# Decoding FP4 weight codes during attention and keeping the scales out of the gate and up products

## The chip, the cores and the metric

The kernel runs on one core of a Trainium2 chip. The metric is the device time of one execution in microseconds (us), as the median of several runs. The core has five engines with queues of their own, in order: TensorE (PE, matmuls), VectorE (DVE), ScalarE (ACT), GpSimd (POOL) and SyncE (SP, which here issues all DMA transfers). They wait for each other through semaphores.

## What is computed

`x` is (16, 100, 512) and the context (16, 361, 512), in float32. First a gated cross attention, then a gated feed-forward network (FFN) with FP4 weights:

```python
x = x + tanh(g_xattn[0]) * xattn(layernorm(x), ctx, mask, norm_w, wq, wk, wv, wo, wg)
x = x + tanh(g_ffn[0]) * ffn(layernorm(x), gate_up_packed, gate_up_scales, down_packed, down_scales)

def ffn(x, ...):                       # I = 1408 hidden, 512 in and out
    w_gu = dequant(gate_up_packed) * scale per (group of 128 inputs, output)
    w_down = dequant(down_packed)  * scale per (group of 128 hidden, output)
    gate, up = split(x @ w_gu.T)
    h = silu(gate) * up
    y = h @ w_down.T
    return y / sqrt(mean(y * y) + 1e-6)
```

A packed word holds eight 4-bit codes with the values 0, 0.5, 1, 1.5, 2, 3, 4, 6 and their negatives. The scales are float16.

## The kernel before

**Precision.** Matmuls run in a float32 format of TensorE with a shorter mantissa. Each operand is therefore kept as two halves, "hi" (rounded, made by ACT) and "lo" (the rest, made by DVE or POOL), and `product` (L254 to L258) issues three matmuls for each tile of 128 inputs: hi with hi, hi with lo, lo with hi (`PASSES`).

**Attention.** The 16 batches go in four groups of four. A group has 16 steps, one per head. `step` exists on PE (L1314), ACT (L689), DVE (L915) and POOL (L548), and each engine goes through its own list in the written order. On DVE a step is: split of the transposed probabilities (`probsT_lo`), normalising of the head before (`attn_norm`), row maxima two steps ahead (`row_max`), layer statistics of the next group in steps 6 to 9, splits of the projections that PE computes beside this step (`job_lo`, or `output` for the jobs O), normalising. The list `BESIDE` says which jobs stand beside which step: X (transposed input), Q, K, A and B (values), T (transposed head outputs), G (gate), O (output projection). Step 12 has X2, X3 and Q0 of the next group, and Q0 needs all X splits. The steps run in a loop over the first three groups (from step 6 of one group to step 5 of the next); the last ten steps, of the fourth group, are written out behind it, followed by T3, O0 to O3 and four `output` calls (L904 to L912), each of which ends in a tile of x1 that SP stores in DRAM (L393) and needs a residual tile `xa` that SP loads (L376).

**FP4 weights.** 17 pieces: 11 of gate and up (one hidden tile each, 128 gate and 128 up columns) and 6 of down. `decode` (L977 to L1023) has five stages, all on DVE: cut the scale (L992, L1011), shift the words (L995, L1000, L1003), take the magnitude (L1014), put in the sign (L1018), and multiply the codes, read as float16, by the two parts of the scale (L1021 for hi, L1023 for lo). Pieces 0 to 8 are decoded in steps 7 to 15 of the last group (`EARLY_AT`), the others between the hidden tiles of the FFN's first token group.

**FFN.** 1,600 tokens in five token groups of 320. Per token group: statistics and normalising of x1 on DVE (L1032 to L1046), transposing on PE (L1343), splitting into `mT` hi and lo (L727, L1053); then 11 hidden tiles, each with two products of 12 matmuls (`gate_up`, L1435), tanh on ACT (L799), gating and multiplication by up on DVE (`hidden_tile`, L1170 and L1173, both reading a PSUM bank), hi on ACT (L803), lo on POOL (L606). Then `down` (L1450): two or three tiles of up to 128 tokens, each with 11 x 3 matmuls of 512 columns, a square with sum on ACT (L810), mean on DVE (L1181), reciprocal root on POOL (L612), scale and residual on DVE (L1184, L1188). Gate and up use two pairs of banks in turn. PE does the down tiles of a token group between two groups' gate and up products. ACT waits for all of x1 to be stored after the first token group.

Of the kernel before, what the change touches and what calls it, by code (L numbers as in the profile page):

```python
# [9 lines left out]
ALU = mybir.AluOpType  # L10
# [3 lines left out]
B, L, D = 16, 100, 512  # L14
# [4 lines left out]
NB = 4  # L19
# [24 lines left out]
PAIRS = (FGROUPS - 1) // 2  # L44


OUT_TILES = ((64, ((64, 128),)), (192, ((192, 128),)), (0, ((0, 64), (TG, 64))), (128, ((384, 128),)), (256, ((512, 128),)))
TILES_OF = ((0, 1), (2, 3, 4))
FP4_UNIT = 16384.0
MASKED = 1e30  # L50
PIECES = FT + 6
# [3 lines left out]
def build(nc, x, ctx_tail, ctx_full, mask, mask_tail, g_xattn, g_ffn, norm_w, wq, wk, wv, wo, wg,  # L55
          gu_packed, gu_scales, dn_packed, dn_scales, identity, shifts, x1_dram, out):
    es = ExitStack()
    with es:
# [8 lines left out]
        shift = sb(es, "shift", [128, 5], I32)  # L67
# [52 lines left out]
        gate = [sb(phase_a, f"gate{b}", [L, D], F32) for b in range(NB)]  # L120
        phase_a.close()

        words = [sb(phase_b, f"words{s}", [128, D], I32) for s in range(2)]
        scale = [sb(phase_b, f"scale{s}", [128, D], F16) for s in range(2)]
        scale_a = [sb(phase_b, f"scale_a{s}", [128, D], F16) for s in range(2)]
        scale_b = [sb(phase_b, f"scale_b{s}", [128, D], F16) for s in range(2)]
        fp4 = [sb(phase_b, f"fp4_{s}", [128, D], I32) for s in range(2)]

        wgu = [[sb(phase_b, f"wgu{t}_{half}", [128, KT, 256], F32R) for half in ("hi", "lo")] for t in range(FT)]
        xb = sb(phase_b, "xb", [128, 3, D], F32)  # L130
        mT = [sb(phase_b, f"mT_{half}", [128, KT, TG], F32R) for half in ("hi", "lo")]
        hT = [sb(phase_b, f"hT_{half}", [128, FT, TG + 64], F32R) for half in ("hi", "lo")]
        tgate = sb(phase_b, "tgate", [128, TG], F32)
        hidden = [sb(phase_b, f"hidden{s}", [128, TG], F32) for s in range(2)]
        wdn = [[sb(phase_b, f"wdn{c}_{half}", [128, 2 if c < 5 else 1, D], F32R) for half in ("hi", "lo")] for c in range(6)]
        mn = [sb(phase_b, f"mn{m}", [128, D], F32) for m in range(3)]

        yo = [words[s][:, :].bitcast(F32) for s in range(2)]
        xr = [fp4[s][:, :].bitcast(F32) for s in range(2)]
# [12 lines left out]
        s_shift = sem("shifts_loaded")  # L152
# [39 lines left out]
        s_words = [sem(f"words_loaded{s}") for s in range(2)]  # L192
        s_scale, s_scaleb, s_shifted = sem("scale_cut"), sem("scale_last_bit"), sem("codes_shifted")
        s_dec = sem("piece_decoded")
        s_whi, s_wlo = sem("ffn_weight_hi"), sem("ffn_weight_lo")
# [4 lines left out]
        s_gu, s_tg, s_sg, s_h, s_hhi, s_hlo = (sem(n) for n in ("gate_up_ready", "tanh_gate", "silu_gate", "hidden_ready", "hidden_hi", "hidden_lo"))  # L200
        s_y, s_sq, s_ms, s_rr, s_cy, s_yo = (sem(n) for n in ("y_ready", "y_squared", "mean_square", "rrms_ready", "coef_ready", "out_ready"))
# [12 lines left out]
        def words_loaded(n):  # L214

            return sum(16 * (4 if m < FT else (5 if m - FT < 5 else 2)) for m in range(n % 2, n + 1, 2))

        def piece_operands(n, half):
            codes, factor = fp4[n % 2][:, :].bitcast(F16), (scale_a if half == HI else scale_b)[n % 2]
            if n < FT:  # L220
                out_ap = wgu[n][half][:, :, :].rearrange("p (two r) c -> p two r c", two=2)
                code = codes.rearrange("p (r c two) -> p two r c", r=2, two=2)
                factor = factor[:, 0:256].unsqueeze(1).unsqueeze(1).broadcast_to([128, 2, 2, 256])
                return out_ap, code, factor
            tiles = 2 if n < PIECES - 1 else 1
            code = codes.rearrange("p (c two) -> p two c", two=2)
            return (wdn[n - FT][half][:, :, :], code[:, 0:tiles, :],
                    factor[:, :].unsqueeze(1).broadcast_to([128, tiles, D]))

        def tile_bank(par, m):  # L230

            return bank[4 + m] if m < 2 else bank[2 * par + 1]

        def hidden_cols(par):

            return slice(64 * par, 64 * par + TG)

        def tile_rows(i, last):
            return 64 if last and i == 2 else 128

        def tile_transfers(h, i, last=False):

            tiles = [m for m in range(i % 2, len(OUT_TILES), 2)]
            per_pair = sum(len(OUT_TILES[m][1]) for m in tiles)
            upto = sum(len(OUT_TILES[m][1]) for m in tiles if m <= i)
            return per_pair * h + (upto - 1 if last and i == 2 else upto)
# [35 lines left out]
        EARLY_AT = {i: i - 7 for i in range(7, STEPS)}  # L282
        EARLY = len(EARLY_AT)
# [67 lines left out]
        def _(sp):  # L351
# [21 lines left out]
            sp.dma_start(shift[:, :], shifts).then_inc(s_shift, 16)  # L373

# [13 lines left out]
            def outputs(g, last):  # L388
                for b in range(NB):
                    if last and b < 3:  # L390
                        load_piece(EARLY - 1 + b)
# [5 lines left out]
                    elif not last:  # L397
                        load_residual(g + 1, b - 2)

            def load_piece(n):  # L400
                s = n % 2
                if n >= 2:
                    sp.wait_ge(s_scaleb, n - 1)
                    sp.wait_ge(s_dec, n - 1)
# [1132 lines left out]
```

## Time and profile before

| | us |
|---|---|
| median of 3 runs | 723.25 (722.58 to 727.46) |
| time of the profiled execution | 725.4 |
| its span, first to last instruction | 723.5 |
| PE busy | 636.1 (88%) |
| DVE busy | 374.2 (52%) |
| ACT busy | 224.6 (31%) |
| POOL busy | 110.9 (15%) |

The span runs from the first to the last instruction of the profiled execution. A row of a group of instructions gives their total and mean duration; engines work side by side, so busy times don't add up to the span. The chain of waits is the sequence of work that ended last, followed back from the end. Matmuls are pipelined: one lasts longer than the distance to the next, so that the chain's time over its count is what one costs. "PEclk" is TensorE's granted clock as a share of 2.4 GHz; 0.50 is 1.2 GHz.

### The profile page before, as it was taken

How to read it: one execution, taken by the hardware profiler on the slowest of the kernel's cores; microseconds unless marked ns; L12 is line 12 of the kernel's file. 1: busy time of each engine (PE TensorE's matmuls, PEld its weight loads, DVE VectorE, ACT ScalarE, POOL GpSimd, SP SyncE). 2: the span in 40 equal slices, each digit the busy share in tenths (PEclk: the TensorE clock that was granted, in tenths of full speed). 3: DMA queues.
4: the chain of work that ended last, by engine and by line, in shares of the span. 5: the costliest groups of instructions: out<-in, count | busy, mean ns of one | idle time of the engine just before them, and what ended most of it. 6: DMA issues, size and time to landing. Idle time of an engine off the chain costs nothing.

```text
span 723.5 us, 12567 instructions
## 1 busy us (share of the span) xinstructions
PE 636.1 (88%) x4594; PEld 574.9 (79%) x4594; DVE 374.2 (52%) x836; ACT 224.6 (31%) x645; POOL 110.9 (15%) x132
## 2 busy tenths in 40 slices
PE   1699979999789989899546877999999999999997
PEld 1598869888788868788434767899989989989994
DVE  6745535565455654567995899422422242242221
ACT  2754445334453453433210011212202212221210
POOL 5710120002100030000000011212201211221220
PEclk9988979999799998999856998999999999999999
DMA  8330020110201100021120311220022001011001
GB/s 274 134 96 3 1 92 1 35 58 0 91 0 45 45 0 0 0 73 60 31 63 5 110 66 42 67 94 1 1 60 66 1 29 65 0 29 58 0 0 44
DMA packets 20178, 33.34 MB, mean 46 GB/s; under 512 B 2988, under 2 KB 6700, under 8 KB 20140
## 3 DMA queue, kind: packets, MB, share of 16 engines
q1 hardware_dynamic: 20140, 32.85, 14.5%
q8 instruction: 22, 0.36, 0.2%
q14 instruction: 16, 0.13, 0.1%
HBM read 26.29 MB, written 6.55 MB: 45 GB/s over the span
## 4 chain that ended last, share of the span: by engine, by line
PE 65%; DVE 19%; ACT 6%; issue 6%; POOL 1%; DMA 1%; SPq 1%; ACTq 0%; DVEq 0%; POOLq 0%
PE bank L258 43%; PE bank L1458 13%; PE bank L1310 3%; ACT probs L678 3%; DVE nmax L886 2%; PE bank L1286 2%; DVE wgu_lo L1023 2%; DVE pT_lo L891 2%; DVE vb_lo L854 2%; ACT vb_hi L658 1%; PE bank L1297 1%; DVE fp L1018 1%; DVE wgu_hi L1021 1%; DVE fp L1014 1%; PE bank L1343 1%
## 5 line engine op out<-in xcount | busy, mean ns | idle before, releaser
L258 PE MATMUL bank<-mT_hi,wgu_hi 128*128 128x320 f32 x440 | 138.6, 315 | 10.2 <-DVE hidden L1173 8.9
L258 PE MATMUL bank<-mT_lo,wgu_hi 128*128 128x320 f32 x440 | 137.9, 313 | 0.0
L258 PE MATMUL bank<-mT_hi,wgu_lo 128*128 128x320 f32 x440 | 137.8, 313 | 0.0
L678 ACT ACTIVATE probs<-bank,nmax 100x96 f32<-100x96 f32 x256 | 66.1, 342 | 132.4 <-DVE nmax L886 132.4
L258 PEld LDWEIGHTS bank<-mT_hi,wgu_hi 128*128 128x128 f32 x440 | 84.3, 192 | 11.9 <-issue 10.3
L258 PEld LDWEIGHTS bank<-mT_lo,wgu_hi 128*128 128x128 f32 x440 | 84.5, 192 | 0.2
L1170 DVE SCALAR_TENSOR_TENSOR hidden<-tgate,bank 128x320 f32<-128x320 f32 x55 | 26.8, 487 | 111.8 <-ACT tgate L799 111.8
L258 PEld LDWEIGHTS bank<-mT_hi,wgu_lo 128*128 128x128 f32 x440 | 84.3, 192 | 0.0
L606 POOL TENSOR_TENSOR hT_lo<-hidden,hT_hi 128x320 fp32r<-128x320 f32 x55 | 49.9, 908 | 189.6 <-ACT hT_hi L803 189.6
L799 ACT ACTIVATE tgate<-bank 128x320 f32<-128x320 f32 x55 | 24.0, 437 | 168.0 <-PE bank L258 139.9
L1458 PE MATMUL bank<-wdn_hi,hT_hi 128*128 128x512 f32 (+1 forms) x143 | 56.2, 393 | 0.0
L1458 PE MATMUL bank<-wdn_lo,hT_hi 128*128 128x512 f32 (+1 forms) x143 | 55.8, 390 | 0.0
L1458 PE MATMUL bank<-wdn_hi,hT_lo 128*128 128x512 f32 (+1 forms) x143 | 55.7, 389 | 0.0
L1310 PE MATMUL bank<-vb_hi,pT_hi 128*100 128x68 f32 x192 | 51.1, 266 | 4.0 <-DVE o L901 3.8
L1310 PE MATMUL bank<-vb_lo,pT_hi 128*100 128x68 f32 x192 | 51.0, 266 | 0.0
L1310 PE MATMUL bank<-vb_hi,pT_lo 128*100 128x68 f32 x192 | 50.8, 265 | 0.0
L891 DVE TENSOR_TENSOR pT_lo<-bank,pT_hi 128x300 fp32r<-128x300 f32 x64 | 29.9, 468 | 31.0 <-ACT pT_hi L686 30.3
L1297 PE MATMUL bank<-ident,probs 100*128 100x100 f32 x192 | 29.2, 263 | 13.8 <-DVE pT_lo L891 13.8
L854 DVE TENSOR_TENSOR vb_lo<-bank,vb_hi 32x256 fp32r<-32x256 f32 (+2 forms) x56 | 23.7, 422 | 31.7 <-ACT vb_hi L658 27.9
L1310 PEld LDWEIGHTS bank<-vb_hi,pT_hi 128*100 128x100 f32 x192 | 34.4, 179 | 5.9 <-DVE pT_lo L891 3.5
L545 POOL TENSOR_TENSOR rstd<-var,halfpow 100x1 f32<-100x1 f32 x16 | 9.1, 566 | 191.5 <-DVE var L876 191.5
L1297 PEld LDWEIGHTS bank<-ident,probs 100*128 100x128 f32 x192 | 23.2, 149 | 19.1 <-issue 15.0
(129 smaller groups left out, 1415.4 us busy)
## 6 DMA issues: line engine op xcount, KB each, us to landing
xn<-in_x SPq DMA_DIRECT2D x16, 200.0 KB
xa<-in_x SPq DMA_DIRECT2D x16, 200.0 KB
x_scratch<-gate SPq DMA_DIRECT2D x16, 200.0 KB
ctx_raw<-in_ctx_tail SPq DMA_DIRECT2D x4, 768.0 KB, 6.9
xb<-x_scratch SPq DMA_DIRECT2D x5, 512.0 KB, 3.9
fp<-x_scratch SPq DMA_DIRECT2D x10, 256.0 KB, 2.7
out_x<-words SPq DMA_DIRECT2D x10, 256.0 KB, 2.1
words<-in_dn_packed SPq DMA_DIRECT2D x6, 256.0 KB
```

What stands on the lines that cost most here:

```text
L258: last = nc.tensor.matmul(out_ap, lhs(a, t), rhs(b, t), start=t == 0 and p == 0, stop=t == tiles - 1 and p == 2)
L606: nc.gpsimd.tensor_tensor(hT[LO][:, t, hidden_cols(par)], hidden[(par + t) % 2][:, :], hT[HI][:, t, hidden_cols(par)].bitcast(F32), ALU.su ...
L678: last = nc.scalar.activation(probs[i % 2][:, cols], SC[i % HPG][0:L, cols], ACT.Exp, bias=nmax[:, i % 4, b:b + 1])
L799: nc.scalar.activation(tgate[:, :], bank[2 * ((par + t) % 2)][:, 0:TG], ACT.Tanh, scale=0.5 * FP4_UNIT).then_inc(s_tg, 1)
L854: last = nc.vector.tensor_tensor(value_cols(name, LO, rows, blk), src[rows, 0:HALF].rearrange("p (h d) -> p h d", d=HD), value_cols(name, ...
L886: nc.vector.tensor_reduce(nmax[:, i % 4, :], SC[i % HPG][0:L, 0:KC].rearrange("t (b k) -> t b k", b=NB), AXIS_X, ALU.max, negate=True).the ...
L891: nc.vector.tensor_tensor(pT[i % 2][LO][:, :, :].rearrange("k c t -> k (c t)"), PT[:, 0:CHUNKS * L], pT[i % 2][HI][:, :, :].rearrange("k c ...
L1023: nc.vector.tensor_tensor(*piece_operands(n, LO), ALU.mult).then_inc(s_wlo, 1)
L1170: nc.vector.scalar_tensor_tensor(tile[:, :], tgate[:, :], 1.0, gate_bank[:, 0:TG], ALU.add, ALU.mult)\
L1297: last = nc.tensor.transpose(PT[:, L * c:L * c + L], probs[i % 2][:, CHUNK * c:CHUNK * c + CHUNK], ident[0:L, 0:L])
L1310: last = nc.tensor.matmul(PV[0:L, VW * c:VW * c + 2 * VW].rearrange("t (b w) -> t b w", w=VW), pT[i % 2][ph][:, c, :], vb[vh][:, c, :, VW ...
L1458: last = nc.tensor.matmul(bank[6 + slot][0:rows, :], hT[a][:, t, col:col + rows], wdn[t // 2][b][:, t % 2, :], start=t == 0 and p == 0, st ...
```

## The change

- **Weights.** The gate and up weights are now the bare codes (exact in one half). Each of the four groups of 128 inputs has its own product: two matmuls (hi and lo of the input) into a bank of its own, from a ring of five banks. The scales, one per group and hidden unit, are pointer scalars (`scale32`) when the products are taken out of the banks.
- **Sums.** Of the eight products of a hidden tile ACT takes out three (gate 0 and 1, up 0: `scale_product`, a scaled copy into SBUF). DVE adds the other five (`scale_add`): gate 2 onto gate 0, gate 3 onto gate 1, and up 1, 2, 3 onto up 0, in a chain. POOL adds the two gate sums (`gate_sum`). Then tanh on ACT, gating on DVE (`gated`) and, one tile later, the multiplication by up (`times_up`), now all between SBUF tensors.
- **Decoding.** The pieces are decoded in the attention loop, six in each of the first three groups, in steps 8 to 13 (`PIECE_AT`, kinds u d u u d u): a gate/up piece is shift, magnitude, sign and a cast to float32; a down piece still gets both parts of its scale. Each result of 512 KB goes to DRAM (`keep_piece`) and is loaded back during the fourth group (`load_gate_up`, `load_down`). No decoding is left in the fourth group and in the FFN.
- **Order.** Statistics, normalising, transposing and splitting of token group 0 move into steps 12 to 15 of the fourth group. In the FFN the loops are written out; statistics of the next token group stand beside hidden tiles 0 to 2, normalising (four operations of 128 columns for each former one) beside 3 to 5, transposing beside 5 to 7. Down products of the token group before stand beside the hidden tiles of this one, two or three chunks (of 3 matmuls) each. ACT starts the FFN only when all of x1 is stored; the load of x1 for token group 1 is issued after that.

The core of the diff (its loops over `j` and `t` are, in this order, POOL's, ACT's, DVE's and PE's):

```diff
+KINDS = "uduudu"
+PIECES = len(KINDS) * (GROUPS - 1)
...
-        EARLY_AT = {i: i - 7 for i in range(7, STEPS)}
+        PIECE_AT = {8 + q: q for q in range(len(KINDS))}
+        STATS_AT, TURNED_AT = 12, {13: 0, 14: 1, 15: 2}
+        ROUND, TURNED = (2, 3, 4, 5, 0), bank[1]
+        TURN_AT = (5, 6, 7)
...
+            def gate_sum(j, t):
+                n = FT * j + t
+                a, b = part[n % 2][0]
+                pool.wait_ge(s_ed, 5 * n + 2)
+                nc.gpsimd.tensor_tensor(a[:, :], a[:, :], b[:, :], ALU.add).then_inc(s_gate_sum, 1)
...
+            for j in range(FGROUPS):
+                for t in range(FT):
+                    for n in tiles_done(j, t):
+                        rms_tile(n)
+                    gate_sum(j, t)
+                    if t == 2 and j + 1 < FGROUPS:
+                        ffn_rstd(j + 1)
+                    if t:
+                        hidden_lo(j, t - 1)
...
+            act.wait_ge(s_stored, 1)
+            for j in range(FGROUPS):
+                for t in range(FT):
+                    for n in tiles_done(j, t):
+                        square(n)
+                    for k in range(2):
+                        scale_product(j, t, 0, k)
+                    scale_product(j, t, 1, 0)
+                    if t:
+                        hidden_hi(j, t - 1)
+                    if t in TURN_AT and j + 1 < FGROUPS:
+                        mT_hi(j + 1, TURN_AT.index(t))
+                    tanh_gate(j, t)
...
+            def scale_add(j, t, i, k):
+                n = FT * j + t
+                onto = part[n % 2][i][k - 2 if i == 0 else 0][:, :]
+                dve.wait_ge(s_gu, 2 * KT * n + KT * i + k + 1)
+                dve.wait_ge(s_ea, 3 * n + (k - 1 if i == 0 else 3))
+                if i == 1 and k > 1:
+                    dve.wait_ge(s_ed, 5 * n + 1 + k)
+                nc.vector.scalar_tensor_tensor(onto, product_bank(j, t, i, k)[:, 0:TG], scale32[:, t, i, k:k + 1], onto,
+                                               ALU.mult, ALU.add).then_inc(s_ed, 1)
...
+            for j in range(FGROUPS):
+                for t in range(FT):
+                    for n in tiles_done(j, t):
+                        mean_square(n)
+                    for k in (2, 3):
+                        scale_add(j, t, 0, k)
+                    if t:
+                        times_up(j, t - 1)
+                    if j + 1 < FGROUPS:
+                        if t < 3:
+                            ffn_stats(j + 1, t)
+                        elif t < 6:
+                            ffn_normalise(j + 1, t - 3)
+                    for k in (1, 2, 3):
+                        scale_add(j, t, 1, k)
+                    gated(j, t)
+                    for n in tiles_done(j, t):
+                        output_tile(n)
+                    if t in TURN_AT and j + 1 < FGROUPS:
+                        mT_lo(j + 1, TURN_AT.index(t))
...
+                for k in range(KT):
+                    open_bank_of(FT * j + t, KT * i + k)
+                    for half in (HI, LO):
+                        last = nc.tensor.matmul(product_bank(j, t, i, k)[:, 0:TG], wgu[t][:, k, 128 * i:128 * i + 128], mT[j % 2][half][:, k, :],
+                                                start=half == HI, stop=half == LO)
+                    last.then_inc(s_gu, 1)
...
+            for j in range(FGROUPS):
+                for t in range(FT):
...
+                    chunks = chunks_beside(j, t)
+                    products(j, t, 0)
+                    for n, c in chunks[:1]:
+                        down(n, c)
+                    products(j, t, 1)
+                    for n, c in chunks[1:]:
+                        down(n, c)
```

## Rows read from the trace of the kernel before

**Rows 1.** Busy time by stretch: start and end, length, then each engine's busy us, clock.

```profile
480.00:520.00 40.00, 40.00 (x262) 39.12 (x261) 13.04 (x30) 8.71 (x22) 10.54 (x12) 1.00 0.10 31
...
459.80:723.50 263.70, 258.38 (x1533) 238.00 (x1532) 81.09 (x181) 50.68 (x129) 50.95 (x63) 1.00 0.10 31
```

**Rows 2.** Chain of waits in order of time: start us, us, what.

```profile
388.20 0.68 PE bank L1258 x4
...
476.29 38.72 PE bank L258 x264
515.00 7.51 PE bank L1458 x33
522.51 1.27 PE bank L1343 x12
```

**Rows 3.** Busy time by stretch again (PE, PEld, DVE, ACT, POOL, clock, DMA): attention, one between-groups stretch.

```profile
240.20:325.40 85.20, 78.00 (x698) 69.63 (x697) 46.63 (x119) 38.01 (x120) 7.68 (x9) 0.94 0.07 19
...
330.70:388.20 57.50, 33.35 (x241) 28.61 (x240) 54.53 (x122) 13.24 (x45) 1.24 (x1) 0.73 0.12 36
...
516.50:526.80 10.30, 10.30 (x52) 8.45 (x51) 6.79 (x17) 2.41 (x6) 2.56 (x4) 1.00 0.04 9
...
248.60:281.70 33.10, 28.50 (x223) 25.02 (x222) 16.11 (x43) 15.37 (x47) 7.02 (x8) 0.85 0.00 0
...
254.70:259.70 5.00, 5.00 (x53) 4.12 (x52) 3.28 (x9) 3.16 (x11) 0.81 (x2) 1.00 0.00 0
...
268.40:277.80 9.40, 6.52 (x26) 6.08 (x26) 2.83 (x7) 2.83 (x10) 2.50 (x2) 0.50 0.00 0
...
245.50:248.60 3.10, 3.10 (x25) 3.06 (x24) 2.25 (x7) 1.68 (x7) 0.10 (x1) 1.00 0.00 0
```

**Rows 4.** Instructions by line and shape: count, busy us, mean ns, idle before.

```profile
L1188 DVE SCALAR_TENSOR_TENSOR words<-bank,coef_y,fp 128x512 f32<-128x512 f32 x12 | 9.0, 751 | 1.5 <-DVE coef_y L1184 0.3
...
L908 DVE SCALAR_TENSOR_TENSOR gate<-gate,bank 100x512 f32<-100x512 f32 x16 | 11.0, 688 | 20.5 <-PE bank L258 20.5
...
L1173 DVE SCALAR_TENSOR_TENSOR hidden<-hidden,bank 128x320 f32<-128x320 f32 x55 | 26.8, 487 | 1.9
...
L799 ACT ACTIVATE tgate<-bank 128x320 f32<-128x320 f32 x55 | 24.0, 437 | 168.0 <-PE bank L258 139.9 <-DVE hidden L1170 28.1
...
L803 ACT ACTIVATE hT_hi<-hidden 128x320 fp32r<-128x320 f32 x55 | 25.6, 465 | 3.7 <-DVE hidden L1173 3.6
...
L606 POOL TENSOR_TENSOR hT_lo<-hidden,hT_hi 128x320 fp32r<-128x320 f32 x55 | 49.9, 908 | 189.6 <-ACT hT_hi L803 189.6
```

**Rows 5.** Timelines of DVE and POOL: start us, us, engine, line, operation.

```profile
31.04 2.72 DVE L842 SCALAR_TENSOR_TENSOR wg_lo<-wg_raw,normw,wg_hi 128x512 fp32r<-128x512 f32 x4
...
418.21 1.11 DVE L1014 TENSOR_SCALAR fp<-words 128x512 int32<-128x512 int32 x1
...
417.95 1.09 POOL L606 TENSOR_TENSOR hT_lo<-hidden,hT_hi 128x320 fp32r<-128x320 f32 x1 [2.59 <-ACT hT_hi L803]
```

**Rows 6.** Instructions by line and shape again: the stages of decode on DVE.

```profile
L1014 DVE TENSOR_SCALAR fp<-words 128x512 int32<-128x512 int32 x17 | 11.3, 662 | 0.0
...
L1003 DVE TENSOR_SCALAR words<-words,shift 128x512 int32<-128x512 int32 x5 | 2.4, 481 | 0.0
...
L1018 DVE SCALAR_TENSOR_TENSOR fp<-words,fp 128x512 int32<-128x512 int32 x17 | 11.8, 692 | 0.5
...
L1021 DVE TENSOR_TENSOR wgu_hi<-fp,scale_a 128x1024 fp32r<-128x1024 f16 x11 | 13.4, 1221 | 0.2
```

**Rows 7.** One line's instructions: duration in ns, shortest, median and longest.

```profile
L844 DVE TENSOR_TENSOR wk_lo<-wk_raw,wk_hi x4: 678/1108/1494, 21.6 to 25.0; 128x512 fp32r<-128x512 f32 x4
```

**Rows 8.** DVE's timeline at the last x1 tile, and the loads of xb (KB, us to landing).

```profile
404.85 0.75 DVE L912 SCALAR_TENSOR_TENSOR gate<-gate,coef_a,xa 100x512 f32<-100x512 f32 x1 [0.74 <-DMA xa<-in_x]
...
xb<-x_scratch SPq DMA_DIRECT2D x5, 512.0 KB, 3.9
```

More of the change, by code:

```diff
@@ L120, in build @@
         gate = [sb(phase_a, f"gate{b}", [L, D], F32) for b in range(NB)]
-        phase_a.close()
[L123 to L129, printed above, removed]
+        words = [sb(phase_a, f"words{s}", [128, D], I32) for s in range(2)]
@@ L212, in wait_apart, with product_bank, ring, chunks_beside @@
             engine.sem_inc(s_apart, 1)
[L214 to L246, printed above, removed]
+        ROUND, TURNED = (2, 3, 4, 5, 0), bank[1]
+        TURN_AT = (5, 6, 7)
+        def product_bank(j, t, i, k):
+            return bank[ROUND[(2 * KT * (FT * j + t) + KT * i + k) % len(ROUND)]]
+        def ring(first, count):
+            return slice(first % RING, first % RING + count)
+        def chunks_beside(j, t):
+            chunks = [(n, c) for n in TILES_BESIDE[j] for c in range(FT)]
+            per = len(TILES_BESIDE[j])
+            return chunks[per * t:per * t + per]
+        def tiles_done(j, t):
+            if t == 0:
+                j, t = j - 1, FT
+            return [n for n, c in chunks_beside(j, t - 1) if c == FT - 1] if j > 0 else []
         def phase_barrier(engine):
@@ L695, in step @@
                         job_hi(*job)
+                if last and i in TURNED_AT:
+                    mT_hi(0, TURNED_AT[i])
                 if not last:
@@ L929, in step @@
                     layer_stats(g + 1, NORM_AT[i])
-                if last and i == STEPS - 1:
-                    ffn_stats(0)
+                if last and i == STATS_AT:
+                    for m in range(3):
+                        ffn_stats(0, m)
                 dequant(3)
@@ L940, in step @@
                 dequant(4)
-                if last and i == STEPS - 1:
-                    for m in range(3):
+                if last and i == STATS_AT:
+                    ffn_normalise(0, 0)
+                elif last and i == STATS_AT + 1:
+                    for m in (1, 2):
                         ffn_normalise(0, m)
+                if last and i in TURNED_AT:
+                    mT_lo(0, TURNED_AT[i])
             for b in range(NB):
@@ new lines, in down @@
+            def down(n, c):
+                rows, slot = OTILES[n], n % 2
+                cols = ring(128 * n, rows)
+                if c == 0 and n >= 2:
+                    pe.wait_ge(s_yo, n - 1)
+                if n == 0 and c == 0:
+                    pe.wait_ge(s_wdn, 16 * 2 * FT)
+                pe.wait_ge(s_hlo, FT * ((128 * n + rows - 1) // TG) + c + 1)
+                for p, (a, b) in enumerate(PASSES):
+                    last = nc.tensor.matmul(bank[6 + slot][0:rows, :], hT[a][:, c, cols], wdn[c][b][:, :],
+                                            start=c == 0 and p == 0, stop=c == FT - 1 and p == 2)
+                last.then_inc(s_dn, 1)
```

600 lines of the change are left out of this document (298 added, 302 removed).

## The prediction

> **What bounds the kernel now.** I read the busy time by stretch first. Over the middle of the FFN TensorE is busy for 40.00 of 40 us at full clock and DVE for 13.04; from the first down projection to the end TensorE works 258.4 of 263.7 us [rows 1]. The chain of waits says the same: one token group's gate and up products are 264 matmuls in 38.72 us (0.147 each), one down tile 33 in 7.51 (0.228 each), a group's transposes 1.27 [rows 2]. So there only fewer matmuls help, until another engine is full. The stretches before it look different. In an inner loop period of 85.2 us (16 attention steps) TensorE is busy 78.0 and DVE 46.6, but the last ten steps, which carry ten of the FP4 pieces, take 57.5 us with DVE busy 54.5: DVE bounds those [rows 3]. They end where the chain reaches T3 at 388.20 [rows 2].
>
> **The FFN products.** With bare codes as weights each group of 128 inputs needs two passes, not three: 176 matmuls of 0.147 = 25.8 us per token group, 12.9 less, 64.5 over five. The down work stays at 13 tiles (about 97 us), now interleaved from the second token group on. TensorE per hidden tile: 16 x 0.147 = 2.35 us in token group 0; with two or three down chunks of 0.68 beside it 3.7 or 4.4. Per token group, transposes included: 27, 43, 50, 43, 48 us; then 22.5 for the last three tiles.
>
> **What takes their place on DVE.** Per hidden tile DVE gets five scaled adds (a product bank, a pointer scalar and an SBUF sum), the gating and the multiplication by up. The nearest row to a scaled add is L1188: 0.751 us for 512 columns; 192 fewer columns, worth the 0.20 between L908 and L1173 without a pointer, make 0.55 [rows 4]. Operations without a wait between them overlap: four of 512 columns start to end in 2.72, so (2.72 - 0.75)/3 = 0.66 apart, 0.46 for 320 [rows 5]. The three up adds form a chain, each waiting for the last, so two of them cost 0.55 + 0.03. The sum is four independent steps of 0.46, two of 0.58 and two of 0.40 for gating and multiplication (0.49 long [rows 4]): about 3.4 us where DVE now spends 1.0. ScalarE has three scaled copies at about 0.53 (tanh's 0.437 plus a pointer), tanh and hT_hi, 2.5 us; POOL two sums at 0.91, 1.8 [rows 4]. Neither fills.
>
> The two operations with two SBUF inputs now run beside a busy POOL. L1014 started at 418.21 while POOL's hT_lo ran from 417.95 to 419.04, and lasted 1.11; its mean over 17 is 0.66 [rows 5, 6]. L844, two SBUF inputs, ranges from 0.68 to 1.49 in the stretch where POOL splits the context [rows 7]. So the one waits for the other. Timed out by hand: the multiplication starts just before POOL's gate sum and pushes it back; hT_lo follows the gate sum and ends about 3.6 after the previous gating, which then waits for it. I take **3.6 us a tile**, 3.4 and 4.2 (a wait of nearly a POOL operation in every tile) being the bounds.
>
> The Trainium skill (SBUF — State Buffer, section "SBUF: two separate sides") states that POOL and a DVE operation with two SBUF inputs exclude each other for a whole instruction. By that rule the tile comes to 3.6, without it to 3.4; L1014's row agrees, and no row shows the FFN's own pair.
>
> Per token group DVE also has statistics, normalising (now 12 operations of 128 columns) and mT_lo. The gap between token groups, DVE busy 6.8 in 10.3 us, holds these and one output tile's 1.1 [rows 3]; I take 6.5. Work ahead of the up adds gives POOL its time, so the 0.2 of port wait drops out of six tiles: 11 x 3.6 - 1.4 + 6.5 = 44.7. An output tile costs 2.0, not 1.1, since DVE waits there for the square and ScalarE's first copy comes after it. Against TensorE: group 0 44.7 (DVE); group 1 47.5 (DVE); group 2 54, where the two are level (51 and 50) and their peaks fall in different tiles; group 3 49.5; group 4 52, TensorE's 48 plus three output tiles. **248 us.** The tail adds 22.5 + 1 and the unchanged end: 5.3 us, the part of the last stretch in which TensorE has nothing left to do [rows 1].
>
> **The pieces, moved into the first three groups.** One up piece is shift 0.48, magnitude 0.42 to 0.66, sign 0.69, cast 0.7 to 1.22: 2.5 us. A down piece has two more operations over 1,024 scales (about 1.1) and two products of 1.22: 5.1 [rows 6]. Four and two of them: 20.5 us per loop, in steps 8 to 13. Those take 33.1 us with DVE busy only 16.1 [rows 3], so the sum would fit; the order does not. DVE's queue is rigid: behind shift and magnitude waits row_max, behind it the exponentials and pT_hi, behind the sign and cast the xT split, behind that Q0 on TensorE. Step 9 (5.0 us, DVE 3.3) gets a down piece: 8.4 busy, about 7.3 with overlap, moving G3 and the next pT_lo. Step 12 (9.4 us, clock 0.50) is a chain of transposes, xT_hi, xT_lo, Q0; its down piece pushes 2.7 us of stages ahead of xT_lo. Walking all six steps, the first pT_hi after them comes 7 to 8 us later; with POOL's context splits colliding with the casts 8.3. Bounds: nothing (all hidden) and 20.5 x 0.85 = 17. I take 8.3, nearer the row that shows free DVE time: **+25 us** over three loops.
>
> The Trainium skill (VectorE: DVE Perf Modes, "The perf-mode tier table") puts an SBUF copy at twice the rate of a two-input operation. The cast would then be 0.7 and the piece near 2.3; no row of before shows it, and the three loops would lose 22 instead of 25.
>
> The stores and loads (8 x 512 KB per loop, then 11 MB of weights during the last group) go in SP's queue between waits for the steps; SP and the DMA engines are nearly idle there [rows 3], and I cost them at nothing. If they are late, the first to notice is the cast, then the x1 loads behind them.
>
> **The last ten steps without pieces.** Step 7, one product beside it, takes 3.1 us with DVE at 2.25 [rows 3]. Steps 7 to 10 stay with their products (3.1 + 6.0 + 4.6 + 4.5); 11 is 3.2; 12 and 13 get the FFN's statistics and normalising (5.9, 4.1); 14 and 15 one transposed tile each (2.5, 3): 37.5 for 57.5, **-20**. T3 moves from 388.2 to 393.
>
> **The step into the FFN.** From T3 to the last x1 tile 17.4 us pass: the last operation of output waits for its residual and ends at 405.6 [rows 8]. ScalarE now starts only when that tile is stored, about 3 us more, at T3 + 20.5 = 413.7. The loads of xb for token group 1 are issued after it too and take 3.9 [rows 8]. DVE's in-order queue holds the first statistics, and behind them the up adds that free the banks: +3.3.
>
> **Sum:** 388.2 + 25 - 20 + 20.5 + 3.3 + 248 + 23.5 + 5.3 = 693.8 against the profiled span of 723.5, which lies within 0.3 of the median of the runs: **694 us**.
>
> **Rivals.**
> - The pieces hide. DVE is half idle in steps 8 to 13 [rows 3]; against it stands the queue order. 694 - 25 = 669. Chance 0.12.
> - TensorE stays the bound in the FFN, because DVE overlaps more than I allow (3.4 or less a tile): 212 for 248 at the extreme, half of it likely: 676. Against it are five adds of at least 0.46. Chance 0.12.
> - Slower, one mechanism: port turns. If both two-input operations wait out a whole POOL operation, a tile takes 3.4 + 2 x 0.9 = 5.2, and 55 tiles cost up to 88 more: 780. It decides from about 4.15 a tile, where the gain of 29 is gone. For it: L844's 1.49 [rows 7]; against it: POOL has only two short operations per tile. Chance 0.07.
> - TensorE, 60% busy in group 0, falls to half clock, as in step 12 [rows 3]: a tile then needs 4.7, +9: 703. Or late weights and stores hold T3 or the start by some 10: 704. Chance 0.18 together.
> - The forecast itself, 684 to 706 with its own small errors: 0.51.
>
> A range of 674 to 715 leaves out the far ends of the first three. A run within 1% of before can't be told from no change. Faster by over 1% (under 716): 0.85; within: 0.08; slower: 0.07.
>
> **What would show it.** The tanh of successive tiles 3.6 to 3.9 us apart in token group 0; the gating longer than 0.49 where hT_lo runs; scaled adds of 0.55; TensorE about 60% busy in group 0 and over 90% in groups 2 and 4; loop period near 93.5, T3 near 393, ScalarE's first scaled copy near 414. A tile over 4.2, or a loop period over 100, would make the prediction wrong; so would a start of the FFN later than 425.

## The result: slower, and the profile after

| | before | after |
|---|---|---|
| median of the runs | 724.12 us (722.58 to 727.46, 4 runs) | 740.32 us (736.85 to 742.29, 4 runs) |
| span of the profiled execution | 723.5 | 740.5 |
| PE busy | 636.1 | 610.5 |
| DVE busy | 374.2 | 509.4 |
| mean granted clock of PE | 0.935 | 0.892 |

After over before is 1.021, 95% interval 1.018 to 1.024. The forecast of 694 us was wrong by 46 us, and so was its sign.

The first view is the busy time by stretch of the changed kernel (columns as in [rows 1] and [rows 3]): the second period of the attention loop; then the hidden tiles of token groups 0 to 4, each stretch from the end of the one before it; then the tail.

```profile
174.70:270.70 96.00, 81.40 (x699) 72.01 (x699) 66.01 (x148) 37.81 (x120) 9.26 (x10) 0.89 0.31 100
...
425.90:484.40 58.50, 41.98 (x187) 34.17 (x188) 46.11 (x98) 26.92 (x59) 20.50 (x22) 0.82 0.10 32
484.40:542.70 58.30, 47.75 (x256) 41.79 (x255) 48.05 (x104) 27.67 (x62) 22.29 (x24) 0.94 0.07 21
542.70:603.10 60.40, 53.09 (x284) 46.04 (x284) 49.92 (x110) 28.36 (x63) 23.49 (x26) 0.97 0.12 38
603.10:665.10 62.00, 51.60 (x261) 45.02 (x260) 49.27 (x106) 28.76 (x65) 22.86 (x25) 0.89 0.06 18
665.10:713.00 47.90, 47.90 (x271) 43.55 (x270) 40.21 (x87) 27.03 (x60) 22.76 (x25) 1.00 0.10 34
713.00:740.50 27.50, 22.15 (x98) 16.15 (x96) 5.25 (x14) 2.91 (x9) 3.26 (x5) 0.94 0.15 48
```

The loop period is not 85.2 as in [rows 3] nor the forecast 93.5, but 98.2, 96.0 and 98.2. In the FFN, groups 0 to 3 take 58 to 62 us each, and in none of them is any engine full: DVE, the fullest in group 0, is busy for 46.1 of 58.5; PE, the fullest in group 2, for 53.1 of 60.4. Only group 4, which has no token group to prepare, has PE busy for its whole 47.9, as nearly all of the FFN of before had [rows 1]. So something that stands only in the groups that prepare the next one makes two engines wait for each other. The waits of PE in the FFN (waiting engine, result and line, what it waited for: us in total, times, longest) name it:

```profile
PE bank L1411 <- DVE mT_lo L1098: 27.2, 8, 5.2
PE bank L1522 <- DVE part_up L1216: 13.8, 19, 2.1
PE bank L1522 <- ACT part_gate L832: 3.6, 1, 3.6
PE bank L1522 <- DVE part_gate L1216: 0.6, 2, 0.3
```

L1411 are the transposes of the next token group's input, L1098 DVE's split of the transposed tile before. Eight times, twice in each of four groups, they wait, for 27.2 us. One such place on DVE's timeline:

```profile
454.78 2.26 DVE L1090 TENSOR_SCALAR mn<-xb,mv,rstd 64x128 f32<-64x128 f32 x4
456.92 1.90 DVE L1216 SCALAR_TENSOR_TENSOR part_up<-bank,scale,part_up 128x320 f32<-128x320 f32 x3
458.74 0.48 DVE L1224 SCALAR_TENSOR_TENSOR hidden<-tgate,part_gate 128x320 f32<-128x320 f32 x1
459.14 0.68 DVE L1098 TENSOR_TENSOR mT_lo<-bank,mT_hi 128x512 fp32r<-128x512 f32 x1
462.63 1.08 DVE L1216 SCALAR_TENSOR_TENSOR part_gate<-bank,scale,part_gate 128x320 f32<-128x320 f32 x2 [2.81 <-PE bank L1522]
```

and on PE's:

```profile
454.39 0.31 PE L1522 MATMUL bank<-mT_lo,wgu 128*128 128x320 f32 x1
459.88 1.12 PE L1411 MATMUL bank<-ident,mn 128*128 128x128 f32 x4 [5.18 <-DVE mT_lo L1098]
460.64 0.62 PE L1522 MATMUL bank<-mT_hi,wgu 128*128 128x320 f32 x1
461.06 0.47 PE L1522 MATMUL bank<-mT_lo,wgu 128*128 128x320 f32 x1
```

PE runs one hidden tile ahead of DVE. Its transposes go into one bank (`TURNED`), so those of tile m need the split of tile m - 1, and that stands at the very end of DVE's hidden tile, behind normalising, the up adds and the gating. PE stands 5.18 us with the next tile's products queued behind the transposes. Once the split is done, DVE has nothing left to do and waits 2.81 us for these products, whose matmuls now start 0.27 us apart (0.15 before the wait): the granted clock is 0.50 from 459.9 to 464.0 and was 1.00 from 450.8 to 454.7. Overlap is lost in both directions, at the second and third of the three neighbouring tiles in `TURN_AT = (5, 6, 7)`, in each group.

### The profile page after: what moved, and what is told of

Its sections match the earlier page's. It is cut to its first block, busy times and chain, and to the rows that moved or that the text cites. A ratio compares the mean times of both kernels' runs of the same rounds, so it can differ in the third digit from the quotient of the medians.

```text
span 740.5 us, 12443 instructions
## 1 busy us (share of the span) xinstructions
PE 610.5 (82%) x4154; PEld 531.4 (72%) x4154; DVE 509.4 (69%) x1117; ACT 306.8 (41%) x810; POOL 170.5 (23%) x187
## 4 chain that ended last, share of the span: by engine, by line
PE 49%; DVE 29%; issue 9%; ACT 8%; POOL 3%; DMA 1%; DVEq 1%; ACTq 0%; SPq 0%; POOLq 0%
PE bank L258 19%; PE bank L1522 13%; PE bank L1535 10%; DVE mn L1090 4%; DVE part_up L1216 3%; PE bank L1372 3%; ACT probs L713 3%; DVE nmax L930 2%; DVE part_gate L1216 2%; DVE xn L925 2%; DVE pT_lo L935 2%; PE bank L1348 2%; DVE vb_lo L898 1%; ACT vb_hi L693 1%; DVE words L1033 1%
## 5 line engine op out<-in xcount | busy, mean ns | idle before, releaser
L1522 PE MATMUL bank<-mT_hi,wgu 128*128 128x320 f32 x440 | 147.5, 344 | 20.5 <-DVE part_up L1216 13.8
L1522 PE MATMUL bank<-mT_lo,wgu 128*128 128x320 f32 x440 | 140.4, 328 | 0.0
L1522 PEld LDWEIGHTS bank<-mT_hi,wgu 128*128 128x128 f32 x440 | 90.2, 205 | 38.5 <-DVE part_up L1216 24.5
L1216 DVE SCALAR_TENSOR_TENSOR part_up<-bank,scale,part_up 128x320 f32<-128x320 f32 x165 | 90.6, 549 | 27.6 <-ACT part_up L832 11.9
L637 POOL TENSOR_TENSOR part_gate<-part_gate 128x320 f32<-128x320 f32 x55 | 57.9, 1052 | 182.9 <-DVE part_gate L1216 182.9
L1522 PEld LDWEIGHTS bank<-mT_lo,wgu 128*128 128x128 f32 x440 | 90.5, 206 | 3.5
L832 ACT ACTIVATE part_gate<-bank,scale 128x320 f32<-128x320 f32 x110 | 52.7, 523 | 69.9 <-PE bank L1522 50.8
L1216 DVE SCALAR_TENSOR_TENSOR part_gate<-bank,scale,part_gate 128x320 f32<-128x320 f32 x110 | 55.8, 545 | 25.0 <-PE bank L1522 17.8
L832 ACT ACTIVATE part_up<-bank,scale 128x320 f32<-128x320 f32 x55 | 29.0, 528 | 74.2 <-PE bank L1522 74.2
L258 PE MATMUL bank<-xT_hi,wq_hi 128*128 128x400 f32 x64 | 26.6, 416 | 18.3 <-DVE xT_lo L901 17.5
L1411 PE MATMUL bank<-ident,mn 128*128 128x128 f32 (+1 forms) x60 | 11.8, 336 | 33.2 <-DVE mT_lo L1098 30.1
```

The lines of the kernel that those rows point to most:

```text
L258: last = nc.tensor.matmul(out_ap, lhs(a, t), rhs(b, t), start=t == 0 and p == 0, stop=t == tiles - 1 and p == 2)
L637: nc.gpsimd.tensor_tensor(a[:, :], a[:, :], b[:, :], ALU.add).then_inc(s_gate_sum, 1)
L832: nc.scalar.activation(part[n % 2][i][k][:, :], product_bank(j, t, i, k)[:, 0:TG], ACT.Copy, scale=scale32[:, t, i, k:k + 1]).then_inc(s_e ...
L1216: nc.vector.scalar_tensor_tensor(onto, product_bank(j, t, i, k)[:, 0:TG], scale32[:, t, i, k:k + 1], onto, ALU.mult, ALU.add).then_inc(s_e ...
L1522: last = nc.tensor.matmul(product_bank(j, t, i, k)[:, 0:TG], wgu[t][:, k, 128 * i:128 * i + 128], mT[j % 2][half][:, k, :], start=half == ...
```

## Experiments

Periods of the attention loop and cycles of a hidden tile (from one gating L1224 to the next) are differences of start times in ScalarE's and DVE's timelines. An attention step runs from its `pT_hi` on ScalarE to the next one.

### Transposing beside tiles that aren't neighbours

```diff
-        TURN_AT = (5, 6, 7)
+        TURN_AT = (5, 7, 9)
```

> The changed kernel with TURN_AT = (5, 7, 9) in place of (5, 6, 7): the three transposed tiles of the next token group stand two hidden tiles apart. Theory A (TensorE's queue is held by a wait that the prediction did not name: a transpose needs the one bank of the tile before, which DVE's mT_lo frees only at the end of its hidden tile, and the products of the next hidden tile stand behind the transpose): the two bubbles per token group go, hidden tiles 6 and 7 fall from 7 to 9 us to about 4.2 to 5, and with four token groups that have them the time falls by 20 to 30, to 710 to 720. Theory B (the long tiles are DVE's own work, or the half clock of TensorE by itself): tiles 6 and 7 stay long or the length moves to tiles 7 and 9, and the time stays within 5 of 740.

Measured: 711.06 us (710.05 to 714.92), 0.983 of before (0.978 to 0.987), against 1.021 of the change itself. PE's waits in the FFN are now

```profile
PE bank L1522 <- DVE part_up L1216: 19.7, 24, 2.2
PE bank L1522 <- ACT part_gate L832: 3.6, 1, 3.6
PE bank L1522 <- DVE part_gate L1216: 1.1, 4, 0.3
```

The wait for `mT_lo` is gone; some of it comes back as waits for the up adds, 19.7 us for 13.8. In group 0 the cycles of tiles 6 and 7 fell from 7.49 and 7.19 us to 4.14 and 3.54, and the time by 29 us. From the first gating to the end, the two profiled executions differ by 28.6 (307.8 and 279.2). Theory A holds. One tuple decides whether the change is slower or faster than the kernel before. Tiles 3 to 5 stay at 5.69.

### Normalising in one operation

```diff
-                for g in range(KT):
-                    cols = slice(128 * g, 128 * g + 128)
-                    last = nc.vector.tensor_scalar(mn[m][0:rows, cols].rearrange("t (e p) -> t p e", e=4),
...
+                nc.vector.tensor_scalar(mn[m][0:rows, :].rearrange("t (g e p) -> t g p e", g=KT, e=4),
+                                        xb[0:rows, m, :].rearrange("t (g p e) -> t g p e", g=KT, e=4), mv[0:rows, m, 0:1],
+                                        rstd[0:rows, m:m + 1], ALU.subtract, ALU.mult).then_inc(s_mn, 1)
```

> The changed kernel with the normalising of a tile as one operation of 512 columns instead of four of 128. Theory A (each short operation in turn waits for the SBUF port that POOL holds, 2.3 us for four beside POOL against 1.17 for four in attention, where POOL is idle): one operation waits at most once, or, if it runs at one element per cycle as in the kernel before (0.73), not at all; hidden tiles 3 to 5 fall from 5.7 to about 4.2 and the time by 12 to 18, to 722 to 728. Theory B (the four operations cost their fixed parts, and POOL has nothing to do with it): tiles 3 to 5 fall by less than 0.6 each, the time by less than 7.

Measured: 726.78 us (721.51 to 731.22, 8 runs), 1.004 of before (1.000 to 1.008). Tiles 3 to 5 went from 5.69 to 4.70 us in group 0 (4.2 had been expected), much the same in the others, 12 tiles in all, and the time fell by 13.5; tiles 6 and 7 still took 7.3 to 9.5 in groups 0, 1 and 3. PE's waits still hold 23.3 us for `mT_lo`, so this is a second cause. DVE's timeline of after shows the four operations of 128 columns where POOL was idle, in the attention: 1.17 us, for 2.26 in the FFN (454.78, above).

```profile
392.38 1.17 DVE L1090 TENSOR_SCALAR mn<-xb,mv,rstd 128x128 f32<-128x128 f32 x4 [1.00 <-POOL rstd L606]
```

The single operation isn't free of it either. In this run it takes 0.75 in the attention and 1.33 in the FFN:

```profile
386.69 0.75 DVE L1088 TENSOR_SCALAR mn<-xb,mv,rstd 128x512 f32<-128x512 f32 x1 [1.00 <-POOL rstd L606]
436.28 1.33 DVE L1088 TENSOR_SCALAR mn<-xb,mv,rstd 128x512 f32<-128x512 f32 x1
```

So of the 0.93 us between 2.26 and 1.33, 0.42 (1.17 to 0.75) goes with POOL idle too, and 0.5 goes with POOL.

### Both together, and whether it is POOL

The two edits above in one kernel:

> Both edits together: transposing beside hidden tiles 5, 7 and 9, and the normalising as one operation of 512 columns. Theory A (two separate costs: the transposed tile's bank is waited for, and each small operation of the normalising waits for the port again): the two gains add. The first gave 29, the second took 1.0 us out of each of tiles 3 to 5 in every group (5.69 to 4.70), 12 tiles: 711 - 12 = 699, with tiles 3 to 5 at 4.7 and tiles 6 to 10 at 3.5 to 4.5. Theory B (what the second edit saved was mainly a shorter wait for the transposed tile, which is gone now): 706 to 711.

Measured: 700.8 us (696.7 to 702.02), 0.967 (0.965 to 0.970). The gains nearly add: 29 and 10. Tiles 3 to 5 take 4.69. From the first gating to the end, after takes 307.8 us, the first edit alone 279.2, the second alone 294.3 and both 267.4: 28.6, 13.5 and 40.4. The FFN is the better place to compare them, since the three attention periods, whose code these runs share, sum to anything from 286.1 to 292.4.

The next run is the changed kernel with POOL's sum on 8 of its 320 columns, so that the gates come out wrong and all waits stay:

```diff
-                nc.gpsimd.tensor_tensor(a[:, :], a[:, :], b[:, :], ALU.add).then_inc(s_gate_sum, 1)
+                nc.gpsimd.tensor_tensor(a[:, 0:8], a[:, 0:8], b[:, 0:8], ALU.add).then_inc(s_gate_sum, 1)
```

> The changed kernel with POOL's sum of the two gate parts on 8 of its 320 columns (the output is wrong; all waits and counts are kept). Theory A (POOL and DVE's operations with two SBUF inputs, and the normalising's, exclude each other for a whole instruction): with POOL 0.8 us shorter per tile, the shortest cycle of a hidden tile goes from 3.54 to 3.36 to 3.4, and the four normalising operations beside tiles 3 to 5 from 2.3 to 1.4 to 1.8 in all. Theory B (DVE's own time is the 3.54, and the normalising is slow by itself): both stay. Tiles 6 and 7, where the transposed tile is waited for, stay at 7 to 9 us by either.

Measured: 731.79 us in one run. POOL's sum there, in the instructions by line and shape (busy us, mean ns, idle before):

```profile
L637 POOL TENSOR_TENSOR part_gate<-part_gate 128x8 f32<-128x8 f32 x55 | 20.6, 375 | 180.3 <-DVE part_gate L1216 180.3
```

and one normalising on its timeline of DVE:

```profile
440.07 1.71 DVE L1090 TENSOR_SCALAR mn<-xb,mv,rstd 128x128 f32<-128x128 f32 x4
```

With POOL's operation 0.68 us shorter (0.375 for the 1.052 of after), DVE's four take 1.71 instead of 2.26 and tiles 3 to 5 fall from 5.69 to 5.12. The normalising reads one tensor of SBUF, and it still waits for POOL. Theory B falls for it. But the shortest cycle of a hidden tile stays 3.54 in both, so there theory A falls: neither the multiplication by up nor the gating, the two with two SBUF inputs, ever lasts more than 0.49 us in either kernel.

### What the loops pay for

The decoding operations on 8 of their columns:

```diff
-                        nc.vector.tensor_copy(left[m % 2][:, :], code.bitcast(F16)).then_inc(s_left, 1)
+                        nc.vector.tensor_copy(left[m % 2][:, 0:8], code[:, 0:4].bitcast(F16)).then_inc(s_left, 1)
```

(the other seven lines of `decode` likewise; the two result buffers are cleared once before the loop).

> The changed kernel with every decode operation cut to 8 columns, so that the weights are wrong; waits, loads and stores stay. It prices the decoding in DVE's queue against its DMA traffic and waits. If DVE's work is the cost, the three loop periods (98, 96, 98 us) return to 85 to 87 and the time falls by 30 to 37, to about 705. If the traffic of 8 stores per loop or SP's order costs, the periods stay above 92.

Measured: 713.84 us (710.4 to 716.61), 26.5 less than after, where 30 to 37 had been expected. The periods are 91.0, 88.5 and 87.0. That is 25.9 of the 37.0 us that the three loops had become longer: DVE's time is most of their price, but they did not fall to 85.2. DVE's waits between 100 and 370 us hold one that after doesn't have:

```profile
DVE left L1055 <- DMA down_scratch<-left: 9.4, 4, 3.0
```

With quick decoding the results come faster than their stores of 512 KB end, and there are two buffers for them. After has no such wait in this window: there DVE's own decoding is slow enough.

Then the whole of each piece behind everything else in the step:

```diff
                 probsT_lo(g, i)
-                dequant(0)
...
-                dequant(4)
+                for stage in range(5):
+                    dequant(stage)
```

> The changed kernel with all five decode stages of a step at its end, behind row_max, the splits and the normalising. The work on DVE is the same. If the place in the queue matters (row_max, and behind it the exponentials and pT_hi, pushed back by the stages ahead of it), the loop period falls from 97 to about 91 and the time by 15 to 20, to about 722. If only the amount of DVE work matters, period and time stay within 2 and 6 us.

Measured: 757.14 us (755.85 to 759.53), 1.045 of before: 17 us slower, not 18 faster. The periods are 100.8, 102.7 and 102.5. My theory named the right queue and the wrong victim. Step 12's down piece now runs between `qT_lo` and the next split of the probabilities, on DVE's timeline:

```profile
319.56 0.57 DVE L904 SCALAR_TENSOR_TENSOR qT_lo<-bank,qT_hi 128x400 fp32r<-128x400 f32 x1 [4.93 <-ACT qT_hi L699]
320.05 0.48 DVE L1030 TENSOR_SCALAR words<-words,shift 128x512 int32<-128x512 int32 x1
...
323.58 1.22 DVE L1057 TENSOR_TENSOR left<-fp,scale 128x1024 fp32r<-128x1024 f16 x1
324.71 0.46 DVE L935 TENSOR_TENSOR pT_lo<-bank,pT_hi 128x300 fp32r<-128x300 f32 x1
```

`pT_hi` had started at 319.42, so `pT_lo` comes 5.3 us after it, where in after it came 1.8 after (307.47 and 309.23). The steps behind the two down pieces grow: step 10 takes 9.2 us for 7.9, step 13 8.3 for 5.5. Moved as a block, a piece stands whole in front of the next thing that PE waits for; spread through the step, a part of it falls into waits of DVE.

### Where in the loop a piece stands

The next runs stand on the kernel with both FFN edits (700.8 us):

```diff
-        PIECE_AT = {8 + q: q for q in range(len(KINDS))}
+        PIECE_AT = {8: 0, 9: 1, 10: 2, 11: 3, 13: 4, 14: 5}
```

> As e5_turn_norm, and the pieces stand in steps 8, 9, 10, 11, 13 and 14 of the attention instead of 8 to 13; step 12 has none. Theory A (a piece costs what it puts ahead of a split that TensorE waits for, and step 12, a bare chain of transposes, splits and Q0, hides nothing): step 12 goes from 11.9 back to 9.35, steps 13 and 14 take the down piece and an up piece with DVE at 2.1 us of 3.9 and 4.3 before, and come to 7 and 5: 21.5 for 23.6 us over the three steps, some 2 to 3 us per loop, 6 to 9 over three, 690 to 693. Theory B (the loop pays the DVE time of the six pieces wherever they stand): no change, 699.

Measured: 690.57 us (688.38 to 691.06), 0.952 (0.950 to 0.955). Step 12 takes 8.8 to 9.4 us instead of 11.4 to 12.0. PE's waits for the X splits in front of Q0, between 60 and 360 us, first of after, then of this run:

```profile
PE bank L258 <- DVE xT_lo L901: 16.2, 3, 5.4
```

```profile
PE bank L258 <- DVE xT_lo L901: 8.3, 3, 2.8
```

The three periods sum to 281.4 instead of 288.0, which is all of the 6.2 us between the two profiled executions (694.9 and 688.7); the one of the kernel with both edits was the fastest of its five, so the medians lie 10.2 apart. Theory A holds. Next, in place of that line:

```diff
+        PIECE_AT = {8: 0, 10: 1, 11: 2, 13: 3, 14: 4, 15: 5}
```

> As e5_turn_norm, and the pieces stand in steps 8, 10, 11, 13, 14 and 15: neither step 9 nor step 12 has one, and the down piece of step 9 is in step 10. Theory A (place decides): beside what leaving step 12 gives, step 9 has no down piece in front of the normalising, which took 2.22 us beside POOL instead of 0.54 and held the next split of the probabilities back by 4 us: 3 to 4 us per loop, 687 to 690. Theory B (DVE time decides): 699. Against A stands that step 10 has a split of the context on POOL too, so that the lock of the port may only move.

Measured: 701.95 us (701.46 to 705.91), no gain, where theory A had 687 to 690. That is the number of theory B, but not its reason. Steps 8 to 12, now with three pieces, take 32.9 us in the second loop (34.1 with four in the run before), but steps 15 and 0 take 7.6 and 10.3. DVE's timeline there:

```profile
226.19 0.68 DVE L1047 SCALAR_TENSOR_TENSOR fp<-words,fp 128x512 int32<-128x512 int32 x1
230.69 0.69 DVE L1055 CAST left<-fp 128x1024 fp32r<-128x1024 f16 x1 [3.82 <-DMA down_scratch<-left]
231.30 2.17 DVE L898 TENSOR_TENSOR vb_lo<-bank,vb_hi 64x256 fp32r<-64x256 f32 x5
```

and the busy time by stretch:

```profile
221.00:229.00 8.00, 4.18 (x34) 3.53 (x32) 5.37 (x11) 3.66 (x12) 0.00 (x0) 0.91 0.91 293
229.00:239.40 10.40, 7.19 (x36) 7.17 (x36) 4.60 (x11) 2.86 (x9) 0.00 (x0) 0.58 0.20 82
```

The cast waits 3.82 us for a store, while the DMA engines are 91% busy at 293 GB/s; behind it wait the splits of the values, behind these PE, which then works at 0.58. Is it the next group's context, loaded ahead of the stores?

```diff
                     for q in range(4):
                         next_piece(g, q)
-                    load_next(g + 1)
                     for q in range(4, len(KINDS)):
                         next_piece(g, q)
+                    load_next(g + 1)
```

> As e7_spread, but the queue of SP issues the loads of the next group (context, mask, x) after the last piece of the group instead of after the fourth. In e7 the cast in step 15 waited 3.82 us for the store of the down piece before it, while the DMA engines were 91% busy with 293 GB/s, and the steps 15 and 0 took 7.6 and 10.3 us (5.2 and 4.8 with no piece near), twice; in the third loop, where no next group is loaded, 7.2 and 5.8. Theory A (the large loads in front of the stores make the wait): the first two loops become as the third, 5 to 6 us each: 690 to 692 for 702. Theory B (two buffers for eight results are too few at this spacing whatever else is loaded): the wait stays, 700 to 702.

Measured: 698.63 us (694.59 to 702.08), between the two. Step 0 fell to 6.0 to 7.0 us, for 10.3 and 10.9 with the loads early. DVE's waits for stores between 60 and 360 us, first with the loads early, then late:

```profile
DVE left L1055 <- DMA down_scratch<-left: 12.6, 5, 4.8
```

```profile
DVE left L1053 <- DMA down_scratch<-left: 7.1, 3, 3.0
```

The three that are left, of up to 3.0 us, come in step 11, in front of the X splits; they were 1.0 to 1.5 us there with the loads early.

So the loads made the waits in step 15 longer, but two buffers remain too few when an up piece follows a down piece's two results within one short step. That is theory B for this part. How the price divides between the waits and PE's lower clock behind them stays open.

### The context's splits away from the down piece

On top of the run with 690.57:

```diff
-        CTX_AT = {9: (0, 1), 10: (2,), 11: (3,)}
+        CTX_AT = {10: (0,), 11: (1, 2), 12: (3,)}
```

> As e6_no_piece_in_12, and the splits of the next context stand in steps 10 (one), 11 (two) and 12 (one) instead of 9 (two), 10 and 11, on ScalarE and POOL. In step 9 the normalising took 2.22 us while POOL worked through its root and two splits, and 0.54 where POOL was idle, and the next split of the probabilities came 4 us after its pT_hi. Theory A (the port lock is part of the price of the piece in step 9): step 9's normalising falls to 0.54 to 1.1, step 10 goes from 7.93 to 6.3 to 6.8, 3 to 5 us over three loops: 686 to 688. Theory B (the lock only moves to step 10 or 11, where two more such operations stand beside POOL): 690 to 692.

Measured: 685.8 us (685.3 to 690.29), 0.948 of before (0.943 to 0.952). What this removes is on DVE's timeline of after in step 9,

```profile
185.96 1.23 DVE L1053 TENSOR_TENSOR left<-fp,scale_a 128x1024 fp32r<-128x1024 f16 x1
187.10 0.57 DVE L909 TENSOR_TENSOR oT_lo<-bank,oT_hi 128x400 fp32r<-128x400 f32 x1
187.59 2.22 DVE L925 TENSOR_SCALAR xn<-xn,mv,rstd 100x512 f32<-100x512 f32 x1
```

and beside it, on POOL's timeline of after:

```profile
186.02 1.57 POOL L567 TENSOR_TENSOR rstd<-var,halfpow 100x1 f32<-100x1 f32 x1 [5.24 <-DVE var L920]
187.57 1.96 POOL L562 TENSOR_TENSOR ctxT_lo<-ctx_raw,ctxT_hi 128x384 fp32r<-128x384 f32 x2
```

and on DVE's timeline of this run it is

```profile
183.14 0.54 DVE L925 TENSOR_SCALAR xn<-xn,mv,rstd 100x512 f32<-100x512 f32 x1
183.59 1.22 DVE L1060 TENSOR_TENSOR left<-fp,scale 128x1024 fp32r<-128x1024 f16 x1
```

2.22 us beside POOL, 0.54 with POOL idle: so once in each loop of after (2.22 to 2.25), and in no loop of this run. The three periods sum to 277.1, 4.3 less: 2.5 of it in steps 8 to 13, 1.8 in steps 14 and 15, where nothing was edited. The time is theory A's, but it rests on one thing more: three of the four executions had a mean granted clock of 0.940 and took 685.3 to 685.9; the fourth had 0.917 and took 690.29, as long as the run before with 0.917 (690.48). Whether the shorter wait gave the higher clock, no run separates.

This version is the fastest of all, 54 us below the change as it was made and some 40 below the kernel before. The 40 lie behind the attention: from the last tile of x1 to the end before takes 317.9 us and this version 276.9, while that tile comes at 407.2 instead of 405.6. How much of the 41 is fewer matmuls and how much is decoding no longer done there, no run tells apart.

## Why the prediction was wrong, point by point

- **The transposes in the FFN: missing, 27 to 29 us.** The sum added up DVE's and PE's work per token group and took the larger. The step "transposes included: 27, 43, 50, 43, 48" counted their 1.3 us of PE and DVE's split, and not that they share one bank and so tie PE to the end of DVE's previous tile. This wait of 27.2 us, put at nothing, is the step that failed. The diff shows the shared bank (`TURNED = bank[1]`, `mT_lo` as the last line of DVE's loop, three neighbouring tiles in `TURN_AT`), and [rows 2] show transposes in a single block only because in the kernel before they stood between two groups. This alone turned the sign, as the run without it shows.
- **Normalising: missing, 10 to 13.5 us.** It stood inside "I take 6.5" for a token group's additional work, with no wait for POOL. Four operations beside POOL took 2.26 us for 1.17, 1.1 per tile dearer; joining them gave back 0.9.
- **Which operations wait for POOL: wrong ones.** I expected the gating to wait for hT_lo (0.2 us per tile) and named two SBUF inputs as the condition. The multiplication did push POOL's sum back, which takes 1.06 us (median) and 0.87 in the first tile, where no multiplication stands before it. But in the shortest cycle hT_lo ends before the gating starts (480.65 and 480.85), and the gating takes 0.48 in all 55 tiles. What waits is L1090, 2.26 for 1.17, and L925, 2.22 for 0.54, both with one tensor input. The prediction's own row had said so: L1014, with 1.11 us beside POOL [rows 5], has one tensor input, so it did not bear out a rule on two. The rule that I cited (the Trainium skill, SBUF — State Buffer, section "SBUF: two separate sides") names besides two SBUF inputs also a DVE operation in a 2-port performance mode, and that half of it I left out. That L1014, L925 and L1090 ran in such a mode, no view here shows. The half with two inputs the trace bears out: POOL's root took 1.57 us beside DVE's product of the down piece, for 0.56 where it was alone.
- **The pieces in the loops: mechanism right, term too small.** Forecast +25, measured +37: the three loops take 292.4 us for 255.4. (In the profiled executions of the four runs that share this attention they are 31 to 33 longer.) (The eighth step of the fourth group is 35 late, 365.7 for 330.7, as 2 us had been gained ahead of the loops.) The walk through the six steps was nearly right. Steps 8 to 13 take 42.3 us in each loop for 33.0, +9.3 for the forecast's 8.3, and step 12 was as worked out: 2.6 us later to its X splits for 2.7. What was left out comes behind them. Steps 14 and 15, which have no piece, take 13.2, 11.0 and 13.2 us for 9.5, with PE's granted clock at 0.58 and 0.64 in the third loop, where it had stood at 1.00. In other executions of the same attention they take 9.5 to 11.8, so this part varies and a forecast could only have bounded it. The cast was 0.69 us, where the rule of the Trainium skill that I cited (VectorE: DVE Perf Modes, section "The perf-mode tier table") had given 0.7.
- **Last steps of the attention: nearly right.** 40.1 us from there to T3 for 37.5, before 57.5. (They are nine steps with nine pieces, 7 to 15, not ten; the terms written down for them add up to 36.9.)
- **The step into the FFN: right.** ScalarE's first copy came 20.1 us after T3 for 20.5, and the statistics waited 2.75 us for `xb` for 3.3.
- **The hidden tile itself: right in size, by luck.** 3.54 us where nothing else stands beside it, for 3.6; scaled adds 0.55; 4.4 in groups 2 and 4, where PE sets the pace. But the 3.6 was 3.4 of DVE's own work and 0.2 of waiting for POOL, and DVE goes through the 3.54 without a gap or a longer operation. The chained up adds make the difference: they start 0.68 us apart, not 0.58. (The 3.4 itself fits three independent steps of 0.46; with the four that are written it would be 3.8.) With both missing terms taken out (700.8), the time from the first copy to the end is 274 us for a forecast of 280.

One of the shortest cycles on DVE's timeline of after, whose three up adds take 1.91 us and whose two gate adds 1.00:

```profile
477.30 0.48 DVE L1224 SCALAR_TENSOR_TENSOR hidden<-tgate,part_gate 128x320 f32<-128x320 f32 x1
477.70 1.00 DVE L1216 SCALAR_TENSOR_TENSOR part_gate<-bank,scale,part_gate 128x320 f32<-128x320 f32 x2
478.62 0.48 DVE L1231 TENSOR_TENSOR hidden<-hidden,part_up 128x320 f32<-128x320 f32 x1
479.01 1.91 DVE L1216 SCALAR_TENSOR_TENSOR part_up<-bank,scale,part_up 128x320 f32<-128x320 f32 x3
480.85 0.48 DVE L1224 SCALAR_TENSOR_TENSOR hidden<-tgate,part_gate 128x320 f32<-128x320 f32 x1
```

So the 46 us that the forecast missed are these, by the profiled executions: ScalarE's first copy came 12 us late (425.9 for 413.7), which is the attention's part (12 more in the loops than forecast and 3 in its last steps, less 2 gained before the loops); from there to the end after takes 314.6 us and the kernel with both edits 274.2, 40 us for the two missing terms; and the rest of the FFN had been put 6 too high. The rival on the other side, port turns in every hidden tile, named the right resource but the wrong place: not 55 tiles, but 12 tiles and one step of each loop. Of the signs that were to show the prediction wrong, two came: tiles over 4.2 (5.7 to 9.5) and a start of the FFN after 425 (425.9). Fewer matmuls and the decoding moved away from the FFN did pay together: it shows at 685.8, once these waits are gone.

## What to carry to other kernels

When engines get nearly equally full, a sum of busy times per stage is a lower bound and not a forecast: go through the order of two neighbouring tiles, look for every buffer that exists once, and ask at which place in the other engine's list it comes free. Spread work that needs such a buffer over tiles that aren't neighbours, and keep background work out of chains in which the next product waits for a split. Beside a busy POOL, join small DVE operations into one, and keep both engines' large SBUF operations in different steps.

## What the hardware showed that I had not expected

- A DVE operation with a single SBUF tensor and two pointer scalars waits for POOL as well: 0.54 us became 2.22, four of 128 columns 1.17 became 2.26. In reverse POOL's root of 100 values went from 0.56 to 1.57 us beside a DVE product of two SBUF tensors.
- Waits of PE cost twice. After 5.18 us without work the matmuls of 320 columns came 0.27 us apart instead of 0.15, a dozen of them (granted clock 0.50); in the attention, PE's clock was 0.58 in the step behind a late one.
- Stores of 512 KB, which the sum had at nothing, are a limit with two buffers. In the run with pieces in steps 8, 10, 11, 13, 14 and 15 they took 2.6 to 10.0 us to land, and seven waits for them add up to 13.8.
